# Attention: the sum of key and relation for one of four tiles made by TensorE and copied by ScalarE

## The reference

```python
Q = (enh @ Wq + bq).reshape(N, H, D)          # H = 4 heads, D = 64
K = (enh @ Wk + bk).reshape(N, H, D)
V = (enh @ Wv + bv).reshape(N, H, D)
rel = rel_w[edge_relations]
mod_k = K[src] + 0.2 * rel[:, None, :]
scores = jnp.einsum('ehd,ehd->eh', Q[dst], mod_k) / D ** 0.5
ex = jnp.exp(scores - segment_max(scores, dst)[dst])
w = ex / segment_sum(ex, dst)[dst]
agg = segment_sum(w[:, :, None] * V[src], dst)
```

## Time and profile before

| | us |
|---|---|
| median of 3 runs | 3117.74 |
| lowest and highest | 3115.02, 3120.06 |
| the profiled execution | 3112.8 |
| its span | 3111.0 |
| granted TensorE clock, mean of the span | 0.881 |
| first and last gather of the attention | 680.5, 1321.2 |
| first and last L1132 | 692.0, 1332.2 |
| last `add` of the attention starts | 1385.2 |

### The profile page before, as it was taken

One profiled execution on the slowest core, in us unless ns is written; L12 is line 12 of the kernel. 1 busy time (PEld: TensorE's weight loads), 2 busy tenths in 40 slices (PEclk: granted clock), 3 DMA queues, 4 the chain that ended last, 5 costly groups with the idle time before them and its releaser, 6 DMA issues. The chain is left out here.

```text
span 3111.0 us, 47135 instructions
## 1 busy us (share of the span) xinstructions
PE 2348.1 (75%) x13339; PEld 1725.7 (55%) x13339; DVE 2276.0 (73%) x5444; ACT 1405.5 (45%) x5149; POOL 1481.3 (48%) x1404
## 2 busy tenths in 40 slices
PE   6335445237777777753799799999999699999997
PEld 3223223125445454432577566666666488899996
DVE  8877777549999999967888599999999830122221
ACT  1000000003566666673423588888888521233332
POOL 0577777617665656600000466666666007234432
PEclk9966666656898989976899899999999889999998
DMA  4223333298787888833000766666666351422223
GB/s 120 74 70 94 97 92 96 61 103 269 242 252 241 250 242 249 232 96 90 1 1 9 213 206 199 198 197 200 201 199 191 85 190 16 102 38 38 36 37 67
DMA packets 288293, 419.62 MB, mean 135 GB/s; under 512 B 118887, under 2 KB 200651, under 8 KB 287720
## 3 DMA queue, kind: packets, MB, share of 16 engines
q0 software_dynamic: 91456, 234.61, 26.9%
q1 hardware_dynamic: 167218, 180.43, 21.2%
q10 hardware_dynamic: 29366, 1.56, 0.9%
HBM read 358.58 MB, written 61.03 MB: 135 GB/s over the span
## 5 line engine op out<-in xcount | busy, mean ns | idle before, releaser
L1337 POOL DMA_INDIRECT g_rows<-h_d,src x416 | 452.5, 1088 | 637.3 <-POOLq L74 419.0
L989 POOL DMA_INDIRECT a_strip<-kv_d,src x416 | 405.6, 975 | 302.4 <-DVE x L1132 129.6
L330 POOL DMA_INDIRECT rec_d<-o_rec_in,o_place x392 | 391.9, 1000 | 212.5 <-issue 110.1
L1020 ACT ACTIVATE x<-a_strip,x 128x64 f32<-128x64 f32 x1664 | 408.4, 334 | 134.0 <-PE a_psv L1065 133.8
L1065 PE MATMUL a_psv<-x 128*125 128x260 f32 x832 | 284.9, 447 | 128.9 <-DVE agg L1163 118.5
L1435 PE MATMUL g_psa<-g_msg,g_hot 128*125 128x256 f32 x832 | 233.8, 405 | 57.2 <-issue 53.6
L1065 PEld LDWEIGHTS a_psv<-x 128*125 128x125 f32 x832 | 139.9, 200 | 208.3 <-DVE agg L1163 181.2
L1435 PEld LDWEIGHTS g_psa<-g_msg,g_hot 128*125 128x125 f32 x832 | 141.1, 189 | 173.9 <-issue 158.7
L2498 DVE TENSOR_TENSOR e_w1s<-e_psy,e_room 128x256 f32<-128x256 f32 x56 | 23.8, 425 | 290.6 <-PE e_psy L2701 285.5
L2592 POOL DMA_INDIRECT x_d<-e_w1s,e_listed x56 | 110.3, 1970 | 225.7 <-DVE e_w1s L2500 217.9
L1045 PE MATMUL a_psq<-q,a_ht 125*128 x1248 | 199.4, 312 | 21.6 <-DVE a_ht L1123 15.6
(11 more groups left out here) (440 smaller groups left out, 5409.4 us busy)
## 6 DMA issues: line engine op xcount, KB each, us to landing
a_row<-rows_d SPq DMA_DIRECT2D x104, 256.0 KB, 5.5
hot_d<-x SPq DMA_DIRECT2D x104, 250.0 KB, 3.2
g_hot<-hot_d SPq DMA_DIRECT2D x104, 250.0 KB, 2.7
o_row<-dst_rows_d SPq DMA_DIRECT2D x98, 256.0 KB, 3.8
o_row_lo<-lo_rows_d SPq DMA_DIRECT2D x98, 128.0 KB, 4.4
e_w<-in_L_ffn_W1p SPq DMA_DIRECT2D x8, 1024.0 KB
e_w<-in_L_ffn_W2p SPq DMA_DIRECT2D x8, 1024.0 KB
a_strip<-kv_d,src POOLq DMA_INDIRECT x416
```

The lines of the kernel that those rows point to most:

```text
L330: pool.indirect_dma_start(out=m.rec_d[:, :], out_offset=bass.IndirectOffsetOnAxis(ap=place[s % RP][:, u:u + 1], axis=0), in_=rec_in[:, U * ...
L989: pool.indirect_dma_start(out=strip[:, lane.start + u, place:place + 2, :].rearrange("p a d -> p (a d)"), out_offset=None, in_=m.kv_d[:, : ...
L1020: act.activation(msg[b][:, u, h, 0:HD], strip[:, lane.start + u, place, h * HD:(h + 1) * HD], ACT.Copy, scale=w[:, k * U + u, h:h + 1])
L1337: pool.indirect_dma_start(out=rows[r][:, u, 64:576], out_offset=None, in_=m.h_d[:, :], in_offset=bass.IndirectOffsetOnAxis(ap=m.src[:, s * ...
```

## The change

In every step one of the four tiles is taken from VectorE's addition: the last tile in even steps, the first in odd ones (`lifted`). For it TensorE multiplies the relation table with 256 columns (each relation repeated for the four heads) instead of 64, and adds the gathered keys by a float32 product with the identity into the same PSUM columns (`ps_k`, in the half of `ps_r`'s bank that was free). ScalarE copies the result into `kmod` (`lift`), behind twelve of its sixteen scalings. VectorE adds the other three tiles. `kmod` gets a fifth slot, so that the lifted tile alternates between the slots at the two ends and can be written while VectorE still sums the step before; one small tile (`over`) moves out of the shared room to make space. Queries, `multiply` and `total` work as before on all four tiles.

New waits: TensorE's relations wait for the step's gather, for the previous copy (`s_lift`) and, as before, for the previous addition. ScalarE's copy waits for the relations and for `total` two steps back. VectorE's addition waits for the copy. GpSimd waits for the relations too.

```diff
+        kmods = part((U + 1) * D).rearrange("p (u d) -> p u d", d=D)
+        kmod = [kmods[:, 1 - b:1 - b + U, :] for b in range(2)]
+        lifted = [U - 1, 0]
+        added_up = [slice(0, U - 1), slice(1, U)]
...
+        over = sb("over", [H, P])
...
+        ps_k = ps_r[:, U:2 * U, :]
...
                     pool.wait_ge(s_kmod, s - LANE_STEPS + 1)
+                    pool.wait_ge(s_rel, s - LANE_STEPS + 1)
...
                 for u in range(U):
+                    if u == U - 1 and s + LAG + 1 < STEPS:
+                        lift(s + LAG + 1)
...
+            def lift(s):
+                act.wait_ge(s_rel, s + 1)
+                if s >= 2:
+                    act.wait_ge(s_sum, s - 1)
+                act.activation(kmod[s % 2][:, lifted[s % 2], :].rearrange("p (h d) -> p h d", h=H), ps_k, ACT.Copy).then_inc(s_lift, 1)
...
             def relations(s):
+                lane, place = lanes(s)
+                x = lifted[s % 2]
                 if s >= 1:
                     pe.wait_ge(s_kmod, s)
+                    pe.wait_ge(s_lift, s)
-                for u in range(U):
+                for u in range(U)[added_up[s % 2]]:
                     for k in range(3):
...
+                for k in range(3):
+                    pe.matmul(ps_k, ht[s % 2][0:NREL, W + x * EP:W + (x + 1) * EP],
+                              m.rel_b[:, k, None, :].to_broadcast([NREL, H, HD]), start=k == 0, stop=False)
+                pe.wait_ge(s_kv[s % R], 16 * U * (s // R) + 16 * U)
+                pe.matmul(ps_k, m.ident[:, :],
+                          strip[:, lane.start + x, place + 1, :].rearrange("p (h d) -> p h d", h=H),
+                          start=False, stop=True).then_inc(s_rel, 1)
...
+                few = added_up[s % 2]
+                mine = slice(lane.start + few.start, lane.start + few.stop)
+                dve.wait_ge(s_lift, s + 1)
+                dve.tensor_tensor(kmod[s % 2][:, few, :].rearrange("p u (h d) -> p u h d", h=H),
+                                  strip[:, mine, place + 1, :].rearrange("p u (h d) -> p u h d", h=H),
+                                  ps_r[:, few, None, :].to_broadcast([EP, U - 1, H, HD]), ALU.add
+                                  ).then_inc(s_kmod, 1)
```

More of the change, by code:

```diff
@@ L918, in build_attention @@
         ht = [sb(f"ht{b}", [128, 2 * W], BF16) for b in range(2)]
-        kmod = part(U * D).rearrange("p (u d) -> p u d", u=U)
+        kmods = part((U + 1) * D).rearrange("p (u d) -> p u d", d=D)
+        kmod = [kmods[:, 1 - b:1 - b + U, :] for b in range(2)]
+        lifted = [U - 1, 0]
+        added_up = [slice(0, U - 1), slice(1, U)]
         hot = [part(U * P).rearrange("p (u n) -> p u n", u=U) for _ in range(2)]
@@ L930, in build_attention @@
         reach = part(CT + 1)[0:H, :]
-        over = part(P)[0:H, :]
+        over = sb("over", [H, P])
         back = part(CT + 1)[0:H, :]
@@ L948, in build_attention @@
         s_kmod = sem("a_kmod")
+        s_lift = sem("a_lift")
         s_prod = sem("a_prod")
@@ L1022, in weighted @@
                 act.activation(msg[b][:, :, :, HD], w[:, k * U:k * U + U, :], ACT.Copy).then_inc(s_wv, 1)
+            def lift(s):
[3 more added lines that the diff above has]
+                act.activation(kmod[s % 2][:, lifted[s % 2], :].rearrange("p (h d) -> p h d", h=H), ps_k, ACT.Copy).then_inc(s_lift, 1)
+            lift(0)
             for now in range(STEPS + LAG):
@@ L1030, in _ @@
                     weighted(now - LAG)
+                elif now + 1 < STEPS:
+                    lift(now + 1)
                 if now % CS == 1 and 0 <= c < NC:
@@ L1049, in relations @@
             def relations(s):
+                lane, place = lanes(s)
+                x = lifted[s % 2]
                 if s >= 1:
                     pe.wait_ge(s_kmod, s)
-                for u in range(U):
+                    pe.wait_ge(s_lift, s)
+                for u in range(U)[added_up[s % 2]]:
                     for k in range(3):
-                        last = pe.matmul(ps_r[:, u, :], ht[s % 2][0:NREL, W + u * EP:W + (u + 1) * EP],
-                                         m.rel_b[:, k, :], start=k == 0, stop=k == 2)
-                last.then_inc(s_rel, 1)
+                        pe.matmul(ps_r[:, u, :], ht[s % 2][0:NREL, W + u * EP:W + (u + 1) * EP],
+                                  m.rel_b[:, k, :], start=k == 0, stop=k == 2)
+                for k in range(3):
[5 more added lines that the diff above has]
+                          start=False, stop=True).then_inc(s_rel, 1)
             def aggregate(s, half):
@@ L1131, in modify @@
                     dve.wait_ge(s_sum, s)
-                dve.tensor_tensor(kmod.rearrange("p u (h d) -> p u h d", h=H),
-                                  strip[:, lane, place + 1, :].rearrange("p u (h d) -> p u h d", h=H),
-                                  ps_r[:, 0:U, None, :].to_broadcast([EP, U, H, HD]), ALU.add).then_inc(s_kmod, 1)
+                few = added_up[s % 2]
[5 more added lines that the diff above has]
+                                  ).then_inc(s_kmod, 1)
             def multiply(s):
@@ L1138, in multiply @@
                 dve.wait_ge(s_kmod, s + 1)
-                dve.tensor_tensor(kmod[:, :, :], kmod[:, :, :], ps_q[s % 2][:, :, :], ALU.mult).then_inc(s_prod, 1)
+                k = kmod[s % 2]
+                dve.tensor_tensor(k[:, :, :], k[:, :, :], ps_q[s % 2][:, :, :], ALU.mult).then_inc(s_prod, 1)
             def total(s):
@@ L1144, in total @@
                 dve.tensor_reduce(sc[s // CS % 3][:, k * U:k * U + U, :].rearrange("p u h -> p (u h)"),
-                                  kmod.rearrange("p u (h d) -> p (u h) d", h=H), AX.X, ALU.add).then_inc(s_sum, 1)
+                                  kmod[s % 2].rearrange("p u (h d) -> p (u h) d", h=H), AX.X, ALU.add).then_inc(s_sum, 1)
             def one_hot(s):
```

## The result

The changed kernel takes 3097.52 us (median of 4 runs, 3094.99 to 3101.34) against 3116.94 (3115.02 to 3120.06) of the kernel before: ratio 0.9935, 95% interval 0.9922 to 0.9947, 19.4 us less. Two later comparisons of the same kernel gave 0.9928 (0.9914 to 0.9941) and 0.9932 (0.9918 to 0.9945). The forecast, 9.0 us less, was half of what came. The range of the prediction, 3097 to 3122 us, just holds it, and by luck: it is said to begin at rival A's middle, which by A's own ends (3096 and 3102) is 3099. The profiled execution's span is 3095.0 us, 16.0 less than before, though its attention begins 2.05 us later (first gather at 682.51 instead of 680.46), behind stages that the change does not touch.

The account below looks back on a forecast made before the run. VectorE was taken to bound the attention's body. Plain steps -17.6, linking pairs +6.6, start +1 and end +1 gave -9.0 us, a median of 3108 us; range 3097 to 3122 us.

Parts of the forecast that it names:

- rival A: TensorE's clock stays up, so the linking pair costs nothing or gains: 3096 to 3102 us; chance 0.13.
- What bounds it: Attention body: VectorE runs without a gap, so a microsecond off it is one off the span; 0.267 us saved a step.
- Plain steps: Six plain steps in each of eleven chunks: 66 x 0.267 = 17.6 us gained, a step at 5.44 us.
- TensorE's room: Plain steps: TensorE gets 0.84 us more, needs 5.16 of 5.44 us, 0.28 left, so VectorE stays gapless.
- where the gain leaks: Two steps per chunk linking softmax across tiles (a pair), TensorE nearly the bound at low clock: 0.6 us each, 6.6 us lost.
- the upper end: Linking pairs at the low clock throughout: 1.2 us more a pair, 13.2 us over eleven.
- the one-hots' wait for the relations: One-hots now also wait for the identity product, ending about 4.5 us after the previous aggregate's start; VectorE asks at 5.4.
- Start: Attention's start, where gathers set the pace: identity product and copy lengthen the path by 1 to 2 us; 1 us taken.
- End: Attention's last steps: gathers reach TensorE's wait with less room; another 1 us lost.
- Gathers and ScalarE: Plain steps: gathered keys land with 2.9 us left, ScalarE's copy is about 1 us early; neither costs anything.

Follow-up runs that it names:

- e5: The changed kernel with the lifted tile's identity product made twice, so the keys are added twice: 3105.02 us.
- e1: The kernel before with VectorE's addition cut to three tiles, the fourth tile's sum left out, nothing new on TensorE or ScalarE: 3098.51 us, ratio 0.9939.
- e2: The kernel before with the change's TensorE products and gather waits, while VectorE still adds four tiles and nothing is copied: 3115.59 us, ratio 0.9991.
- e4: The changed kernel plus six unread float32 products in TensorE's pause in the first linking step: 3093.47 us, ratio 0.9922; again 3092.68 us, ratio 0.9917.
- e3: The changed kernel with the one-hots' buffer released behind the last product that reads it, not behind the identity product: 3098.55 us.
- e7: The kernel before plus the six idle products in the pause: 3118.39 us, ratio 0.9998.
- e6: The kernel before with VectorE's addition cut to three tiles, plus the six idle products in the pause: 3095.47 us.

## Why the prediction was right and wrong

**What bounds it: right.** VectorE is the bound in the body, and 256 elements less are worth 0.27 us in a plain step: forecast 5.44 us, measured 5.45.

**Plain steps: right, 1 us low.** Six steps a chunk should give 17.6 us and gave 18.6 (1.69 us a chunk in columns 0 and 3 to 7). The surplus is column 6, where three chunks of before had a step of 6.2 us at the low clock and the changed kernel has none.

**TensorE's room: right in its verdict, 0.2 us too small.** +0.84 us was forecast. From the relations' start to the start of an aggregate right behind them it is 1.23 us now; before it was 0.45 at the high clock, where the two stood without a gap (1096.05 to 1096.50 us): 0.8. The identity product takes 0.70 us by itself and 0.43 more when it is made twice (e5, 1.13 for both), so L1435's 0.405 us was the nearer row. The 0.28 us that were to be left are 0.48, mainly since the sum laid durations end to end that overlap: the third aggregate begins at 1057.05 while the identity product's row runs to 1057.21.

**The wrong step: "where the gain leaks".** 0 to 1.2 us a pair were given, 0.6 taken, and 11 x 0.6 = 6.6 us subtracted. Measured: 0.0 us a pair against the kernel before (160.5 us for the eleven pairs in both). Of the 8.5 us between the forecast of -9.0 and the -17.5 of the trace 6.6 are this term; the rest are the plain steps' 1.0 and the end. Three things in it can be told apart. The wait was real: e1 has it, 0.55 us behind queries of 2.74 us, so that the 0.53 us a pair were indeed not to be had without TensorE's work. The extra products were priced at the low clock at 1.7 us and took about 1.5 where they ran at it (2.24 us from 1031.84 to 1034.08, against 0.75 from 1088.54 to 1089.29 in the earlier trace rows). But the upper end held the clock fixed while it lengthened the work that the clock depends on, and no chunk came near it: the costliest kind is 0.2 to 0.4 us above the same chunks before, not 1.2. In eight of eleven chunks the queries' 2.74 us became 1.48 to 2.46, which gave back 0.3 to 1.3 us. The prediction had named this ("the queries give back 1.1 us"), but the middle was taken between "not at all" and "fully" without a reason in the rows. It expected VectorE to wait 12 to 20 us for aggregates, in all eleven places; it waited 3.7 us, and 2.8 of them are the three places of 0.94.

Rival A had the time with a chance of 0.13. As written (clock stays up) it is not what happened either: the clock still falls in every chunk (0.54 and 0.66 in the two short stretches above). It is up again sooner in most; and whether it falls ahead of the relations (2.24 us to the next aggregate) or within them (1.71) decides about 0.6 us, through a wait that the prediction had named as harmless: the one-hots' wait for the relations. In plain steps it was harmless, in five of eleven linking steps it was the one that counted.

**What the clock did.** The trace showed first a pause and then TensorE busy for 7.76 of 8 us at 0.57, and in the changed kernel a pause, then 5.00 of 5.00 us at 0.66; with more work in every step (e2) the body was at 0.96, with the filler in the pause (e4) at 1.00. The Trainium skill (TensorE: Matmul & The Clock Gate, "Part 1: The HAM clock gate") says that activity releases the throttled clock. That agrees with all of this, and the prediction had weighed it against one row of before.

**Start: right.** Forecast +1 us, measured 89.0 - 87.8 = 1.2. The rows landing last now hold up the one-hots by way of the identity product:

```profile
718.41 0.66 DVE L1149 TENSOR_SCALAR a_ht<-a_row,part 128x1024 bf16<-128x1024 bf16 x1 [2.55 <-PE a_psr L1080]
```

(the idle time in brackets is 2.55 us). The price varies: in the other kernels with these products the start takes from 0.5 us (the filler's second trace, 88.3) to 6 us (e5, 93.8) more than before, in e3 and e2 3 us.

**End: half right.** +1 us was forecast. In the first trace of the changed kernel TensorE waited 0.63 us for the last gather, the last step took 5.64 us, and the span behind the last addition is 1778.2 us against 1778.8: nothing. In the second trace the last step took 7.15 us, 1.7 us more than a plain one, for the same reason.

**Gathers and ScalarE: right.** Between 750 and 1320 us TensorE's products waited for gathers 3 times, 2.5 us in all; the copy was never what VectorE waited for. (The 12.8 us at which the identity product asks for its rows are 12.9 by the prediction's own terms, which changes nothing.)

The sum as it came out, in traces: -18.6 for six steps a chunk, 0.0 for the pairs, +1.2 for the start, and 0 (first trace) to +2 (second) for the end; -17.5 in the first trace from first gather to last addition. The medians' 19.4 us lie 2 us beyond it, less than the stages ahead of the attention vary by (its first gather lies between 680.1 and 684.9 us in the thirteen traces).

## What to carry to other kernels

Price added TensorE work at both clocks, and then ask what it does to the clock: a longer busy stretch behind a pause can pay for itself (e2), and a few products that nobody reads inside the pause can be worth more than the shortest possible queue (e4, but not e7). Look at every instance of a place, not at its average: the pairs' unchanged 14.59 us were three kinds. When an engine that is the bound gets shorter, look for the place where it already had no slack (here the aggregate behind the linking), and try the gain alone and the price alone: here the medians moved by -21 and by -4 us, the second hardly clear of nothing, and the change by -23 in the same comparison: the parts don't add up as a gain and a price. A wait that is harmless in nine places can be the one that decides in the tenth, and removing it (e3) only helps if nothing late stands right behind it.

## What the runs showed of the hardware

Six float32 products of 128 columns that nobody reads, 1.50 us in a pause of 1.8, brought the granted clock of 540 us from 0.94 to 1.00 and the kernel 4.9 us down. The same six in the kernel before, with 0.8 us less TensorE work a step, brought the clock from 0.91 to 0.94 and changed the time by nothing (e7), and with the short addition they brought at most 3 us (e6). And 0.8 us of useful work more in each step brought it from 0.91 to 0.96 at no cost in time (e2). Why the filler is enough in the one and not in the others was not settled: the runs show the clock and what TensorE did ahead of it, not the rule between them.
